# Flamingo block on one core: ScalarE issues the shift rows of the next batch, VectorE adds the experts' bias, one transfer spreads the inverses of a half

## The reference

```python
qk = einsum('bdm,bdn->bmn', qh, kh) / sqrt(16)       # b*8 heads, d = 16, m = n = 512
ret = einsum('bmn,bcn->bcm', softmax(qk), vh)
x = x + tanh(g_xattn) * ret.reshape(b, 128, 512)
n = layernorm(x)                                     # 2048 rows of 512
probs = softmax(n @ wg); idx = argmax(probs); gate = probs[idx]
x = x + tanh(g_ffn) * gate * (n @ W[idx].T + bias[idx])
```

## Time and profile before

| what | value |
|---|---|
| median of 3 runs | 586.75 us (580.72 to 587.75) |
| the profiled execution's own time | 586.23 us |
| its span, first to last instruction | 584.6 us |
| PE, DVE, ACT, POOL busy | 88%, 72%, 60%, 60% |
| granted TensorE clock, mean | 0.977 |
| first scores of batch 0 / 1 / 8 / 14 / 15 | 43.5 / 68.5 / 267.4 / 420.0 / 452.2 us |
| slot 8's turn to the end of the last slot's matmuls | 510.8 to 576.2 us |

### The profile page before, as it was taken

How to read it: one execution, slowest core, us unless ns; L and a number is a source line. 1 busy time by engine, 2 the same in 40 slices (tenths; PEclk the granted TensorE clock), 3 DMA queues, 4 the chain that set the end, 5 groups by cost and what they waited for, 6 DMA issues and landing times. The chain is left out here.

```text
span 584.6 us, 9983 instructions
## 1 busy us (share of the span) xinstructions
PE 515.4 (88%) x2603; PEld 183.0 (31%) x2603; DVE 422.7 (72%) x831; ACT 349.7 (60%) x429; POOL 352.5 (60%) x568
## 2 busy tenths in 40 slices
PE   0389999889887999998999999998979979899994
PEld 0012323222323232323333232323322235355551
DVE  5898988768785789888999998989998565112121
ACT  3217887758684778786887877886855842111110
POOL 7444478756564657685767777885473446544532
PEclk9999999989997899999999999999997999999998
DMA  4875457666666486776557555545540154643410
GB/s 141 237 154 178 140 174 201 217 176 185 185 191 176 131 229 197 197 205 175 161 162 213 166 171 153 165 127 158 127 116 24 38 181 163 186 138 98 127 55 0
DMA packets 50392, 90.90 MB, mean 156 GB/s; under 512 B 22018, under 2 KB 24066, under 8 KB 50320
## 3 DMA queue, kind: packets, MB, share of 16 engines
q1 hardware_dynamic: 36096, 65.28, 40.9%
q0 software_dynamic: 10560, 24.93, 12.9%
q10 hardware_dynamic: 3696, 0.23, 0.4%
HBM read 66.91 MB, written 28.41 MB: 163 GB/s over the span
## 5 line engine op out<-in xcount | busy, mean ns | idle before, releaser
L948 DVE TENSOR_REDUCE neg_max<-ps_ring 128x1 f32<-128x512 f32 x480 | 309.0, 682 | 48.9 <-PE ps_ring L1315 47.6
L852 ACT ACTIVATE probs<-ps_scores 128x1024 f32<-128x1024 f32 x256 | 250.1, 1022 | 75.0 <-PE ps_scores L1334 74.2
L1315 PE MATMUL ps_ring<-stacks 96*128 96x512 bf16 x480 | 171.2, 393 | 14.8 <-DVE neg_max L948 13.7
L1334 PE MATMUL ps_scores<-stacks 128*128 128x512 bf16 x512 | 157.1, 390 | 14.9 <-DMA stacks<-shift_parts 8.5
L1357 PE MATMUL ps_pv<-probs,v_ones 128*32 128x512 f32 x992 | 135.2, 618 | 0.0
L1315 PEld LDWEIGHTS ps_ring<-stacks 96*128 96x128 bf16 x480 | 47.1, 98 | 171.4 <-DVE neg_max L948 125.1
L1420 PE MATMUL ps_scores<-w_sb,f_xt 128*128 x184 | 83.2, 593 | 0.0
L1334 PEld LDWEIGHTS ps_scores<-stacks 128*128 128x128 bf16 x512 | 48.2, 102 | 70.4 <-ACT probs L852 21.6
L836 ACT COPY f_xt<-ps_scores 128x512 f32<-128x512 f32 x23 | 13.5, 586 | 72.2 <-PE ps_scores L1401 72.2
L605 POOL CAST shift_parts<-shift 16x128 bf16<-16x128 f32 x32 | 9.0, 282 | 64.6 <-DVE shift L955 64.3
L1420 PEld LDWEIGHTS ps_scores<-w_sb,f_xt 128*128 128x128 f32 x184 | 34.5, 190 | 33.0 <-issue 32.2
(11 more groups left out here) (149 smaller groups left out, 499.8 us busy)
## 6 DMA issues: line engine op xcount, KB each, us to landing
stacks<-parts_dram SPq DMA_DIRECT2D x224, 64.0 KB, 3.0
parts_dram<-prep POOLq DMA_DIRECT2D x15, 768.0 KB, 5.4
w_sb<-w_t SPq DMA_DIRECT2D x16, 512.0 KB, 4.9
recs_dram<-rec SPq DMA_DIRECT2D x16, 512.0 KB, 3.2
stacks<-parts_dram SPq DMA_DIRECT2D x32, 192.0 KB, 3.4
prep<-x_perm SPq DMA_DIRECT2D x16, 256.0 KB, 2.9
prep<-k_perm SPq DMA_DIRECT2D x16, 256.0 KB, 3.2
v_in<-v_t SPq DMA_DIRECT2D x16, 256.0 KB, 3.3
```

The lines of the kernel that those rows point to most:

```text
L852: nc.scalar.activation(probs[:, k % 2, 2 * jp:2 * jp + 2], ps_scores[:, jp], ACT.Exp).then_inc(exp_done, 1)
L948: nc.vector.tensor_reduce(neg_max[:, g, j, c:c + 1], ps_ring[:, SLOT[tile]], AX.X, ALU.max, negate=True).then_inc(ring_free, 1)
L1315: nc.tensor.matmul(ps_ring[:, SLOT[tile]], q_stack[0:KS, into.p, g, j, c * 128:(c + 1) * 128], k_stack[0:KS, into.p, g, j], start=True, st ...
L1334: last = nc.tensor.matmul(ps_scores[:, jp, j % 2], k_stack[0:KA, B.p, g, j, c * 128:(c + 1) * 128], q_stack[0:KA, B.p, g, j], start=True, ...
```

## The change

Parts, in the order of the program:

1. **Shift rows of group 0.** SyncE no longer issues them. ScalarE does, behind both exponentials of step 6 of batch B for batch B+1; for batch 0 it does so after its preparation of batch 1, behind a wait for the padding and for the split maxima, ahead of its preparation of batch 2.
2. **Inverses.** `recip_dram` gets a half for each group with zeros in the other (one store of zeros at batch 0). `spread_recips` becomes one transfer of 256 KB to all 128 partitions. `store_recips(B, 0)` comes ahead of the rows and keys, `spread_recips(B, 0)` behind the values.
3. **Weights**: one piece of 512 KB in each of the 16 batches.
4. **Bias.** `bias_rows`, `bias_parts`, `choose_bias`, their clearing, `split_bias` and the bias matmul go. In batch 14 SyncE loads all eight bias rows, spread over 128 partitions (four transfers of 512 KB), into the half of `stacks` that batch 14 has done with. VectorE adds gate x bias to the record of the next slot behind each combine (`add_bias`), after reading the slot's expert number into a register.
5. **Routing work.** GpSimd's `number_places(1)` and `store_tokens` of batch 14 move behind `add_high` and `rstd2`; `read_slots(0)`, and VectorE's `count_tiles(0)` and `find_blocks(0)`, move from batch 14 to batch 15; `take_columns(0)` moves behind `find_gates(2)`.
6. **Gathers.** From slot 4 on GpSimd issues the gather of slot s+4 ahead of the scatter of slot s.

```diff
@@ SyncE
             def store_recips(B, g):
-                wait(sp, recips_in[g], B.b * (16 * NJ))
+                wait(sp, recips_in[g], B.b * 16)
...
-                sp.dma_start(recip_dram[g].rearrange("j (t c) -> (j t) c", c=DM // 32), sums[:, g]).then_inc(recips_out[g], 16)
+                sp.dma_start(recip_dram[g, :, g].rearrange("j (t c) -> j t c", c=DM // 32), sums[:, g]).then_inc(recips_out[g], 16)
             def spread_recips(B, g):
...
-                for j in range(NJ):
-                    at = 32 * j + g * DH
-                    sp.dma_start(scale[at:at + DH, g], recip_dram[g, j].partition_broadcast(DH)).then_inc(recips_in[g], 16)
+                sp.dma_start(scale[:, g], recip_dram[g].rearrange("j h m -> (j h) m").unsqueeze(1).to_broadcast([NJ * 2, DH, DM])
+                             ).then_inc(recips_in[g], 16)
...
-                if not B.known(NB - 1):
-                    load_shift(B.plus(1), 0)
+                if by_transfer(B):
+                    store_recips(B, 0)
                 if not isinstance(B.b, int) or B.b + 4 < NB:
                     load_rows_keys(B.plus(4))
-                if by_transfer(B):
-                    store_recips(B, 0)
-                    spread_recips(B, 0)
                 if stack:
                     load_stack(B.plus(2), 1)
                     load_values(B.plus(2))
+                if by_transfer(B):
+                    spread_recips(B, 0)
+                if B.known(NB - 2):
+                    for g in range(NG):
+                        sp.wait_ge(scores_ready, B.b * (2 * STEPS) + STEPS * (g + 1))
+                        for s in range(2):
+                            at = (s * NG + g) * 2 * DM
+                            sp.dma_start(biases[:, at:at + 2 * DM], bias[at:at + 2 * DM].partition_broadcast(128)
+                                         ).then_inc(bias_in, 16)
@@ ScalarE
+            def load_shift(B, g):
+                act.wait_ge(shift_ready, B.b * 2 + (g + 1))
...
+                for t in range(NP):
+                    act.dma_start(q_stack[KS + t:KS + t + 1, B.p, g].rearrange("o j (c m) -> o (j c) m", c=NC),
+                                  shift_parts[:, g, t]).then_inc(shift_in[g], 16)
...
+                    if k == 6 and not end:
+                        load_shift(B.plus(1), 0)
@@ VectorE
-                      lambda: nc.vector.memset(bias_rows[:], 0.0),
...
+            def add_bias(s):
...
+                e = nc.vector.value_load(slot_expert[0:1, phase, col:col + 1], min_val=0, max_val=NE - 1)
+                dve.wait_ge(rec_in[r], 16 * (s // NREC + 1))
+                chain.add(nc.vector.scalar_tensor_tensor(
+                    recs_in[r][:, DM:2 * DM], biases.rearrange("p (e n) -> p e n", e=NE)[:, bass.ds(e, 1)]
+                    .rearrange("p o n -> p (o n)"), gate_cols[:, phase, col:col + 1], recs_in[r][:, DM:2 * DM],
+                    ALU.mult, ALU.add))
...
                 combine(s, ps_y[:, s % 2])
+                if s + 1 < NSLOT:
+                    add_bias(s + 1)
@@ TensorE
-                nc.tensor.matmul(bank, choose_bias[:, phase, col:col + 1].to_broadcast([128, 128]), bias_parts[:],
-                                 start=True, stop=False)
@@ GpSimd
-                scatter(s)
+                if s + NREC <= FIRST_LATE:
+                    scatter(s)
...
                 if s + NREC < NSLOT:
+                    wait(pool, y_ready, s + 1)
                     gather(s + NREC)
+                if s + NREC > FIRST_LATE:
+                    scatter(s)
```

More of the change, by code:

```diff
@@ L188, in build @@
         q_stack, k_stack = stacks[:, :, 0], stacks[:, :, 1]
+        biases = stacks[:, 0].rearrange("p s g j m -> p (s g j m)").bitcast(F32)
         v_ones = sb("v_ones", [128, 2, NC, NG, NJ, 2 * DH])
@@ L451, in _ @@
             load_values(Batch(0, 1))
-            sp.wait_ge(pads_in, 16)
-            load_shift(Batch(0, 0), 0)
             load_rows_keys(Batch(1, 1))
@@ L459, in emit @@
                     spread_recips(B.plus(-1), 1)
-                if not isinstance(B.b, int) or B.b < NB // 2:
-                    load_weights(B)
+                load_weights(B)
                 if prev2:
@@ L479, in emit @@
                     load_values(B.plus(2))
-                if B.known(0):
-                    sp.wait_ge(dve_const, BIAS_CLEAR)
-                    for j in range(3):
-                        sp.dma_start(bias_rows[32 * j:32 * j + NE], bias.rearrange("(e n) -> e n", e=NE)
-                                     ).then_inc(bias_in, 16)
+                if by_transfer(B):
[7 more added lines that the diff above has]
+                                         ).then_inc(bias_in, 16)
                 if B.known(1):
@@ L866, in _ @@
                 cast_mid(B)
+                if n == 1:
+                    act.wait_ge(pads_in, 16)
+                    load_shift(Batch(0, 0), 0)
             act.wait_ge(dve_const, DVE_CONSTS)
@@ L1137, in combine @@
                 col = s - PHASES[phase][1]
+                chain.settle()
                 dve.wait_ge(y_full, s + 1)
@@ L1195, in end @@
                 take_maxima(B, ring_base(B) + 1, 1, SLOT["turn1"])
+                count_tiles(0)
+                find_blocks(0)
                 turn_sums(B.plus(-1), 1)
                 invert_sums(B.plus(-1), 1)
-                take_columns(0)
                 take_logits(B.plus(-2))
@@ L1204, in end @@
                 find_gates(2)
+                take_columns(0)
                 add_attention(B.plus(-1))
@@ L1274, in _ @@
             take_columns(1)
+            add_bias(0)
             for s in range(NSLOT):
@@ L1421, in expert @@
                                             w_sb[:, c, bass.ds(e, 1)].rearrange("p o n -> p (o n)"),
-                                            start=False, stop=c == NC - 1)
+                                            start=c == 0, stop=c == NC - 1)
                 last.then_inc(y_full, 1)
```

73 lines of the change are left out of this document (24 added, 49 removed).

## The result

The changed kernel takes 576.44 us (median of 4 runs, 575.28 to 577.69) against 586.6 for the kernel before (4 runs, 580.72 to 587.75): a ratio of 0.986, 95% interval 0.981 to 0.990. That is 10 us less, not 28: the time lies 3 us above the upper end of the range. Of each term I compare the profiled executions (577.69 us, span 576.0, against 586.23 and 584.6).

What follows compares the result with a forecast made beforehand. TensorE was taken as the bound, 24.32 us a batch when nothing is late, with waits and slow clock on top. Shift rows -7.0, clock -8.0, relief -4.0, batch 14 -5.5, batch 15 +1.2, experts -4.1, start -1.0: -28.4, so 558 us (546 to 573).

Steps and rivals of the forecast that it cites:

- One spread of 256 KB in place of four of 32 KB: Spread of the inverses: the wide transfer lands in about 3.5 us, as now; issue time saved pays for the bytes.
- Shift waits and the clock: Early batches: shift rows leaving on ScalarE take back 7.0 us of TensorE waits and 8 us of slow clock behind them.
- SyncE's relief: Batches 1 to 7: fewer SyncE issues and halved weights start stacks, inverses and residual sooner; -4.0 us of TensorE idle time.
- Batch 14: VectorE's thirteen small routing operations leave this batch, taking back 5.5 of its 7.9 us over 24.32.
- Batch 15: Thirteen operations ahead of the turn of batch 14's sums, plus `take_columns(0)` before the second norm: +1.2 us.
- Experts: Sixteen expert slots: no bias matmul saves 3.4 us, earlier gathers net 0.7; together -4.1 us.
- Start: Before the first maxima: clearing `bias_rows` leaves VectorE, -1.0 us.
- B: Inverses' store and spread on fewer DMA engines: each about 1 us longer, 12 us lost over twelve batches, 570; chance 0.12.
- A: Early batches: ScalarE's shift rows land late under load, so wait and slow clock stay; 15 us lost, 573; chance 0.13.
- C: ScalarE stands at the split maxima, delaying step 7's exponentials and TensorE; slower than before, 588; chance 0.03.
- D: VectorE's maxima hold early batches, slow clock comes from elsewhere; only experts, batch 14 and start pay, 578; chance 0.03.
- E: All of it: batches 1 to 14 run near 24.32 + 0.5 us, 13 us more than forecast, 545; chance 0.07.

Runs made afterwards that it cites:

- `rests` first: Changed kernel with GpSimd's `rests` of batch B+3 ahead of `add_low` of batch B-1, nothing else: 556.8 us, ratio 0.956.
- place and form together: Changed kernel with group 0's spread ahead of the second stacks and values, and four 32 KB transfers replacing the wide one: 553.2 us, ratio 0.942.
- the repaired inverses: Changed kernel with group 0's spread early, four 32 KB transfers; the run beside it also put group 0's shift rows back on SyncE: 557.98 us, ratio 0.955.
- part 2 repaired: Changed kernel with early spread and four 32 KB transfers, without (553.2 us) and with (551.38 us) `rests` ahead of `add_low`.
- best version: Changed kernel with group 0's spread early, four 32 KB transfers, and `rests` ahead of `add_low`: 551.38 us, ratio 0.946.
- one twin: Changed kernel with early spread and four 32 KB transfers, shift rows on ScalarE, new store of inverses: 553.2 us, ratio 0.942.
- the other: Changed kernel with early spread, four 32 KB transfers and the old 128x16 store of inverses, shift rows on ScalarE: 555.3 us, ratio 0.952.

## Why the prediction was wrong

**The step that failed** is "One spread of 256 KB in place of four of 32 KB", with the sentence of the part on SyncE that "stacks, inverses and residual start sooner". I took 3.5 us, "as now, since the issue time saved pays for the bytes". Two things were wrong in it. The size: where GpSimd waited for a spread, it started 4.2 us (group 1) and 5.1 us (group 0) after the issue, against 3.3 in the kernel before (medians). And what it left out: the spread of group 0 also moves behind nine stacks and the values, 6.3 us of issues (283.07 to 289.41), so that it starts later, not sooner. The diff showed that move, and I priced only the transfer. I then asked who waits for the inverses of group 1, the one wait that the earlier trace rows had, and not who would wait for those of group 0 or what stands behind that waiter on GpSimd. Together this cost about 20 us: putting `rests` first gives 19.6 of them back by the medians (17 by the ratios), and place and form together 23 (25 by the ratios).

**Batches 8 to 13**: forecast 0, bounds +6 and -6.7; measured +5.5, near the upper bound, by the same chain. With `rests` first they take 152.08, as before (152.62): the added weights cost nothing that shows.

**Shift waits and the clock**: forecast -15 together, all of it put down to the rows' leaving SyncE for ScalarE. The waits did fall by 7.8 (8.5 to 0.7; forecast 7.0), but that is luck for the mechanism: with the rows back in SyncE's queue they are gone as well (none in the changed kernel, 0.2 us beside the repaired inverses), so SyncE's relief by the other parts is enough for it. The move alone, in the kernel before, left 6.2 us of the waits and still took 8 to 10 us off the medians, 13.8 off batches 2 to 7 in its fastest execution. So the relief does most of what I put down to the move: beside the repaired inverses, with the rows in SyncE's queue, batches 2 to 7 take 152.07 us (90.95 to 243.02), 21.5 less than in the kernel before. Of the 10.6 us of slow clock in the early batches only some came back in the changed kernel, since the new waits for exponentials brought slow stretches of their own: TensorE's busy time of batches 2 to 7 fell from 156.56 to 153.19, and to 147.07 once the chain was broken (6 x 24.32 is 145.9).

**SyncE's relief**: forecast -4.0 of idle time. In the changed kernel it is hidden by the chain. With `rests` first batches 0 to 7 take 201.5 us (42.85 to 244.31) against 223.87, -22.4 where -19 was forecast for them. So the sum for these batches was about right once the chain is gone, but not how it splits between the move and the relief.

**Batch 14**: -7.1 against -5.5. **Batch 15**: +5.1 against +1.2; the thirteen operations took 3.8 us, not 2.75, so the wait is 1.96 and not 1.0, and I gave this wait no slow stretch behind it, though I had priced one at all other waits. **Experts**: 3.87 us a slot as forecast; the 1.24 us wait turned into two of 0.50 and 0.75, and in all -2.5 against -4.1. **Start**: -0.7 against -1.0.

**The rivals.** B named the right mechanism, fewer engines per transfer of inverses, at 12 us and a chance of 0.12. It was too small and in the wrong place: it said that `add_high` would wait over 28 us, and that wait fell to 15.2 while a new one of 24.9 rose at `add_low`. It also said nothing of the place in the queue. A is refuted: the shift rows land in 2.1 us (median, 48 transfers), and TensorE waits 0.7 us for them. C is refuted too: the kernel is not slower, and ScalarE's issues lie in its idle time. Its sign, TensorE waiting for exponentials, did come, but without those issues too (18.7 us), so it has another cause. D named 578, nearest to the measured 576.44, but not for its reason: batches 2 to 7 did gain 8.9 us and VectorE's maxima do not hold them (4.4 us of waits). E (545) was 6 to 8 us below what the change does with part 2 repaired (551 to 553).

**What stays open**: why moving the shift rows is worth 8 us against one twin and 2.7 against the other, when no trace of the pair shows a wait for them to speak of; and `high_num` still waits 17.6 us in the best version, which I didn't follow.

## What to carry to other kernels

Where an edit moves a transfer later in a queue, price the move before the transfer: find the first instruction that needs it, and then everything behind that instruction on its in-order engine, even where the profile of before shows no wait there. A wide transfer that replaces several narrow ones should be shaped so that all 16 DMA engines share it, and measured against the narrow ones even so: here four narrow ones with half the bytes were still 2% faster. Where two parts of a change act on the same wait, ask of each whether the other would end it alone. And work for a later batch should not stand behind a wait for an earlier one.

## What the runs showed of the hardware

With the same 256 KB in one or two transfers the kernel took 558, 573 and 627 us on 16, 8 and 4 DMA engines. I had expected that a transfer on fewer engines lands later itself, and it does: 3.6, 4.3 and 5.8 us from issue to use. I had not expected how much it delays small transfers of other queues: the sums of 8 KB, issued by ScalarE, kept VectorE waiting 4.8, 25.1 and 55.8 us. The sums' transfer runs on 4 engines by its 132 packets, 128 runs and 4 completions. That these are among those which the wide transfer fills is my reading of it, which no row shows engine by engine.

Moving three issues of 0.6 us each from SyncE to ScalarE, in the kernel before, took 13.8 us out of six batches in one trace, where the issues themselves take 6 x 1.8 = 10.9. Some 6 to 9 us of the 13.8 is TensorE's busy time, at a granted clock of 1.00 for 0.95. The Trainium skill, page "Trainium Kernel Development and Optimization", section "Key Constraints", says that issuing from several engines saves issue time alone. Issue time saved in a full queue can thus come back with the slow stretches that it ends. Whether it gives more than itself is not shown: that trace is of the fastest execution, and by the medians the whole program gained 8 to 10 us.
